# Two gated layers (state-space scan, quantised FFN, cross-attention, experts) on one core: ScalarE's order of key/value evictions and weight preparation, dummy matmuls at the start, one convolution tap on ScalarE

## The reference

```
x += tanh(g_xattn[0]) * L0_xattn(ctx, layernorm(x))   # in-projection 256->512, causal depthwise
                                                      # convolution (4 taps) + bias, SiLU, x/dt projections,
                                                      # softplus, 16-state scan over 512 steps, * SiLU(z)
x += tanh(g_ffn[0])   * L0_ffn(layernorm(x))          # gate/value/out weights quantised to {-1,0,1}*mean|w|,
                                                      # rows of activations rounded to 127 levels
x += tanh(g_xattn[1]) * L1_xattn(layernorm(x), ctx)   # 16 heads of 128, RMS-normed q and k, softmax, Wo
x += tanh(g_ffn[1])   * L1_ffn(layernorm(x))          # 4 experts, row n goes to expert n % 4, gated
```

## Time and profile before

| what | value |
|---|---|
| median of 3 runs | 1852.88 us (1848.29 to 1855.18) |
| the profiled execution | 1850.82 us |
| its span | 1849.0 us |
| TensorE busy | 1758.0 us (95%) |
| VectorE busy | 1317.9 us (71%) |
| ScalarE busy | 954.9 us (52%) |
| GpSimd busy | 662.6 us (36%) |
| DMA, mean over the span | 158 GB/s |

### The profile page before, as it was taken

The page is one execution under the profiler, slowest core; times in us unless marked ns, Lnnn a source line. Parts: engine busy times, 40 slices in busy tenths (PEclk is TensorE's granted clock), DMA queues, the critical chain, the costliest instruction groups (busy, mean ns, idle before and its releaser), DMA issues.

```text
span 1849.0 us, 19456 instructions
## 1 busy us (share of the span) xinstructions
PE 1758.0 (95%) x6086; PEld 802.9 (43%) x6086; DVE 1317.9 (71%) x1923; ACT 954.9 (52%) x1903; POOL 662.6 (36%) x696
## 2 busy tenths in 40 slices
PE   8989699979999999999999999999999899999999
PEld 3333244434444444444444444444444334455543
DVE  3999987989988798899797988987652444422221
ACT  5979956547554646566445566555435333330100
POOL 2244322246462335457322554562223333310000
PEclk9989899989999999999999999999999999999999
DMA  7999823787851157797213579732112799856210
GB/s 234 255 278 274 248 98 120 178 230 186 207 136 57 50 111 175 183 240 203 65 36 81 143 185 250 201 98 69 35 57 77 220 288 273 238 144 230 83 51 28
DMA packets 159046, 292.11 MB, mean 158 GB/s; under 512 B 18425, under 2 KB 51705, under 8 KB 156001
## 3 DMA queue, kind: packets, MB, share of 16 engines
q1 hardware_dynamic: 141664, 227.95, 39.1%
q0 software_dynamic: 17280, 62.92, 17.7%
HBM read 169.51 MB, written 58.26 MB: 123 GB/s over the span
## 4 chain that ended last, share of the span: by engine, by line
PE 65%; DVE 17%; ACT 6%; issue 5%; DMA 4%; POOL 2%; SPq 1%; DVEq 0%; ACTq 0%; POOLq 0%
PE p L830 10%; PE p L807 8%; PE p L790 8%; PE p L841 8%; PE p L877 6%; DVE s_M L1009 5%; PE p L813 4%; PE p L683 4%; PE p L892 3%; PE p L769 3%; PE p L764 3%; PE p L730 2%; DVE s_M L1004 2%; DVE s_M L1016 2%; DMA s_U<-in_Wq 1%
## 5 line engine op out<-in xcount | busy, mean ns | idle before, releaser
L1154 DVE CUSTOM_DVE_ANT_0 s_U<-p,s_U 128x512 f32<-128x512 f32 x256 | 187.2, 745 | 166.0 <-PE p L807 163.1
L1009 DVE TENSOR_TENSOR_SCAN s_M<-s_M 128x1024 f32<-128x1024 f32 x128 | 296.6, 2317 | 12.0 <-ACT s_M L1266 9.6
L807 PE MATMUL p<-s_U 128*128 128x512 f32 x512 | 267.0, 610 | 4.5 <-DVE s_U L1154 2.4
L790 PE MATMUL p<-s_U 128*128 128x512 f32 x512 | 253.7, 604 | 9.6 <-DMA s_U<-in_Wq 7.0
L1508 POOL DMA_DIRECT2D s_u<-s_M x120 | 113.3, 944 | 400.8 <-DVE s_M L1016 376.0
L1553 POOL TENSOR_SCALAR s_U<-s_U 128x512 f32<-128x512 f32 x256 | 228.6, 913 | 6.3
L841 PE MATMUL p<-s_U 128*128 128x512 f32 x512 | 223.9, 593 | 0.0
L830 PE MATMUL p<-s_U 128*128 128x512 f32 x472 | 213.5, 593 | 2.5 <-ACT s_U L1405 2.5
L1405 ACT COPY s_U<-p 128x512 f32<-128x512 f32 x196 | 105.6, 591 | 187.2 <-PE p L813 185.6
L1266 ACT ACTIVATE s_M<-s_dl,s_small 128x511 f32<-128x511 f32 x256 | 170.2, 717 | 44.2 <-DVE s_M L1009 39.7
L1400 ACT ACTIVATE s_U<-s_U 128x512 f32<-128x512 f32 x256 | 181.6, 710 | 5.3
(11 more groups left out here) (190 smaller groups left out, 2452.7 us busy)
## 6 DMA issues: line engine op xcount, KB each, us to landing
s_u<-s_M POOLq DMA_DIRECT2D x120, 512.0 KB, 7.6
s_bc<-bc_scratch SPq DMA_DIRECT2D x96, 256.0 KB, 4.5
k_scratch<-s_U SPq DMA_DIRECT2D x16, 1024.0 KB, 6.7
v_scratch<-s_U SPq DMA_DIRECT2D x16, 1024.0 KB, 7.4
s_U<-in_Wq SPq DMA_DIRECT2D x64, 256.0 KB, 7.2
s_U<-k_scratch SPq DMA_DIRECT2D x64, 256.0 KB, 5.2
s_U<-rk_scratch SPq DMA_DIRECT2D x64, 256.0 KB, 5.5
s_U<-in_Wo SPq DMA_DIRECT2D x64, 256.0 KB, 4.4
```

The costliest lines, as they stand in the source:

```text
L790: ins = e.matmul(banks[bk][:], wqq[j % 2][:, k, :], axT[b % 2][:, k, :], start=(k == 0), stop=(k == 3))
L807: e.matmul(banks[bk][:], qT[j % 3][:, k * 128:(k + 1) * 128], kT[j % 2], start=True, stop=True).then_inc(S["a_s"], 1)
L1009: e.tensor_tensor_scan(w, dA[i % 2], w, 0.0, ALU.mult, ALU.add).then_inc(S["m_s"], 1)
L1154: e.tensor_tensor_reduce(out=Pm[j % 2][:, k, :], in0=banks[ABANK[kind, j, k]][:], in1=rkb[j % 2], scale=rq[:, k:k + 1], scalar=-3.0e38, op ...
```

## The change: what it does

1. ScalarE's priorities become `AFMKQNE`: all of K, not its first 120 parts, goes ahead of Q, and Q ahead of N.
2. Written durations of some parts are set anew, and `plan()` takes TensorE as free from 7.0 on instead of 0.
3. The FFN's first part `e` no longer waits for all 12 `put`; TensorE's first `m` waits for the first 8, and the waits for all 12 go to the first out matmul and to the first VectorE product. The DMA of the bias rows is issued at `thr` of the last matrix instead of at the last Q part.
4. TensorE begins with 14 dummy matmuls of 128x128 by 128 columns in float32, after the second memset of GpSimd.
5. The convolution's unshifted tap and the bias are computed by ScalarE from PSUM (`Identity` with scale and bias), right after the copy; VectorE keeps three steps of four.

```
-            part((kind, i), [("PE", 1.75), ("ACT", 0.6)], ...)
+            part((kind, i), [("PE", 1.75), ("ACT", 1.25)], ...)
-            part((kind, i), [("DVE", 2.9)], ("in", i))
+            part((kind, i), [("DVE", 2.35)], ("in", i))
...
-                part(name, [("DVE", 2.3)], ("m", t, k - 1), free=pair)
+                part(name, [("DVE", 2.75 if k % 4 == 3 else 1.5)], ("m", t, k - 1), *([] if b else [(0, "put", 2, 3)]), free=pair)
-                part(name, [("PE", 2.6), ("ACT", 0.7)], ("e", t, 2), take=pair)
+                part(name, [("PE", 2.2), ("ACT", 0.7)], ("e", t, 2), *([] if b else [(0, "put", 1, 3)]), take=pair)
-                part(name, [("DVE", 1.0), ("POOL", 1.1)], ("yt", 3), *([] if b else [(0, "put", 2, 3)]))
+                part(name, [("DVE", 1.0), ("POOL", 1.1)], ("yt", 3), *([] if b else [(0, "bias", 0, 2)]))
...
-"s": [("PE", 0.86), ("DVE", 0.9)], "ex": [("ACT", 0.95 if k else 1.35)],  "rc": [("POOL", 1.03 if k else 1.2)]
+"s": [("PE", 0.86), ("DVE", 0.85)], "ex": [("ACT", 0.9 if k else 1.2)],   "rc": [("POOL", 0.95 if k else 1.3)]
...
-FIRST = {..., "ACT": "AFMLQNKE", ...}
+FIRST = {..., "ACT": "AFMKQNE", ...}
+    free["PE"] = 7.0
...
+            def warm():
+                e.wait_ge(S["p_set"], 2)
+                for _ in range(NWARM):                      # NWARM = 14
+                    e.matmul(banks[7][:, 0:128], onesf, onesf, start=True, stop=True)
...
                             if t == 0 and b == 0:
                                 e.wait_ge(S["d_rows"], 32)
-                                e.wait_ge(S["q_put"], 12)
+                                e.wait_ge(S["q_put"], 8)
...
                     elif kind == "l" and k == 3:
+                        if t == 0 and b == 0:
+                            e.wait_ge(S["q_put"], 12)
...
-                        e.tensor_scalar(ac[:, i, :], xs_[:, i, 0:512], cw[:, i, 0:1], cb[:, i:i + 1], ALU.mult, ALU.add).then_inc(*v.up())
-                        for k in range(1, 4):
+                        for k in range(3):
...
                     elif kind == "e" and k == 1:
                         if t == 0 and b == 0:
-                            e.wait_ge(S["q_put"], 12)
+                            e.wait_ge(S["d_rows"], 16)
...
                         e.wait_ge(S["f_th"], i + 1)
+                        if i == 0:
+                            e.wait_ge(S["q_put"], 12)
...
-                        e.copy(xs_[:, i, 3:515], banks[LBANK[b, "in", i]][:]).then_inc(S["m_xs"], 1)
+                        acc = banks[LBANK[b, "in", i]][:]
+                        e.copy(xs_[:, i, 3:515], acc)
+                        e.activation(ac[:, i, :], acc, ACT.Identity, bias=cb[:, i:i + 1], scale=cw[:, i, 3:4]).then_inc(S["m_xs"], 1)
...
-                    if (kind, w, c) == QUANT[-1]:
+                    if (kind, w, c) == ("thr", 2, 0):
                         e.wait_ge(S["q_row"], 1)
                         e.dma_start(brd, rows_).then_inc(S["d_rows"], 16)
```

More of the change, by code:

```diff
@@ L23 @@
 NW = 3
+NWARM = 14
 UW = 27744
@@ L224, in mamba @@
         if kind == "in":
-            part((kind, i), [("PE", 1.75), ("ACT", 0.6)], *([(b - 1, "yt", 3)] if b else []), take=own, free=own)
+            part((kind, i), [("PE", 1.75), ("ACT", 1.25)], *([(b - 1, "yt", 3)] if b else []), take=own, free=own)
         elif kind == "conv":
-            part((kind, i), [("DVE", 2.9)], ("in", i))
+            part((kind, i), [("DVE", 2.35)], ("in", i))
         elif kind == "silu":
@@ L249, in mamba @@
         elif kind == "mul":
-            part((kind, i), [("DVE", 1.25)], *([("out", i - NW)] if i >= NW else []), *([("bc", i // 2)] if b == 0 else []))
+            part((kind, i), [("DVE", 1.23)], *([("out", i - NW)] if i >= NW else []), *([("bc", i // 2)] if b == 0 else []))
         elif kind == "scan":
@@ L253, in mamba @@
         elif kind == "out":
-            part((kind, i), [("DVE", 1.27)] + ([("POOL", 0.8), ("SUM", 5.0)] if i < 2 * NS - 2 else []))
+            part((kind, i), [("DVE", 1.25)] + ([("POOL", 0.8), ("SUM", 5.0)] if i < 2 * NS - 2 else []))
         elif kind == "add":
@@ L347, in context @@
     for kind, j, k in ATTN:
-        does = {"q": [("PE", 0.86)] + ([("ACT", 1.3)] if k == 3 else []), "nq": [("PE", 0.35), ("ACT", 0.4)], "nt": [("PE", 0.2), ("ACT", 0.3), ("POOL", 1.1)], "s": [("PE", 0.86), ("DVE", 0.9)], "ex": [("ACT", 0.95 if k else 1.35)],
-                "rc": [("POOL", 1.03 if k else 1.2)], "tr": [("DVE", 0.65)], "mv": [("DMA", 2.5)], "mr": [("DMA", 4.0)], "t": [("PE", 0.56), ("ACT", 0.6)], "mx": [("PE", 1.73)], "mix": [("PE", 1.73 if halved("mix", j) else 3.45), ("ACT", 0.6)], "wx": [("PE", 1.73)], "w": [("PE", 1.73 if halved("w", j) else 3.45), ("DVE", 0.8)]}[kind]
+        does = {"q": [("PE", 0.86)] + ([("ACT", 1.3)] if k == 3 else []), "nq": [("PE", 0.35), ("ACT", 0.4)], "nt": [("PE", 0.2), ("ACT", 0.3), ("POOL", 1.1)], "s": [("PE", 0.86), ("DVE", 0.85)], "ex": [("ACT", 0.9 if k else 1.2)],
+                "rc": [("POOL", 0.95 if k else 1.3)], "tr": [("DVE", 0.65)], "mv": [("DMA", 2.5)], "mr": [("DMA", 4.0)], "t": [("PE", 0.56), ("ACT", 0.6)], "mx": [("PE", 1.73)], "mix": [("PE", 1.73 if halved("mix", j) else 3.45), ("ACT", 0.6)], "wx": [("PE", 1.73)], "w": [("PE", 1.73 if halved("w", j) else 3.45), ("DVE", 0.8)]}[kind]
         needs = {"q": [(j // NH, "xxt", 3)] + ([] if j else [("K", KV.index((NB - 1, 3, "n", 0)))]), "nq": [(NB, "q", j, 3)], "nt": [(NB, "nq", j, 0)], "s": [(NB, "nt", j, 0)] + ([] if j else [("K", len(KV) - 1)]) + ([(NB, "t" if on_pe(j - 2) else "tr", j - 2, 3)] if j > 1 else []), "ex": [(NB, "s", j, 3)], "rc": [(NB, "rc", j, k - 1) if k else (NB, "ex", j, 3)],
@@ L371, in experts @@
     return out
-FIRST = {"PE": "MNFAQKE", "DVE": "AFQMNKE", "ACT": "AFMLQNKE", "POOL": "MNAFQKE", "DMA": "QMNAFKE", "SUM": "MNAFQKE"}
+FIRST = {"PE": "MNFAQKE", "DVE": "AFQMNKE", "ACT": "AFMKQNE", "POOL": "MNAFQKE", "DMA": "QMNAFKE", "SUM": "MNAFQKE"}
 def plan():
@@ L411, in plan @@
                 ready = max([0.0] + [done[n] + 0.15 for n in needs] + [bank[x] for x in take])
-            key = max(ready, free[e]), FIRST[e].index("N" if s == "M" and name[0] else "L" if s == "K" and e == "ACT" and i < 120 else s)
+            key = max(ready, free[e]), FIRST[e].index("N" if s == "M" and name[0] else s)
             if best is None or key < best[0]:
@@ L898, in tensor @@
                        "K": pe_keys(), "A": pe_attn(), "E": pe_experts()}
+            warm()
             for s in order["PE"]:
@@ L964, in dve_mamba @@
                         e.wait_ge(S["m_xs"], 4 * b + i + 1)
[L965 to L966 removed]
+                        for k in range(3):
                             e.wait_ge(*v.now())
                             ins = e.scalar_tensor_tensor(ac[:, i, :], xs_[:, i, k:k + 512], cw[:, i, k:k + 1], ac[:, i, :], ALU.mult, ALU.add)
[L969 removed]
+                            ins.then_inc(*(v.up() if k < 2 else (S["m_ac"], 1)))
                     elif kind == "soft":
```

1 line of the change is left out of this document (removed).

## The result

The changed kernel takes 1855.34 us (median of 20 runs, 1848.49 to 1861.26), the kernel before 1849.35 (20 runs, 1841.46 to 1855.18). The ratio is 1.0029, 95% interval 1.0016 to 1.0043: slower by some 5 us. That is small, but the interval leaves out 1. The forecast was 1840 and a gain. The profiled execution has a span of 1856.1 us, against 1849.0.

The account below looks back on a forecast made before the run. TensorE, busy for 1758.0 of 1849.0 us, was taken as the bound. 1850.8 - 7 (first product) - 5 (to attention) = 1838.8, plus 2.1 for the runs' median, written 1840; own range 1831 to 1849, stated range 1822 to 1861.

Parts of the forecast that it names:

- Dummy matmuls: At the kernel's start: 28 dummy instructions end at 8.9 us, 1.8 late; gain 1.4 us, bounds 0.1 and 3.2.
- Convolution: Batch 0's four tiles on VectorE end near 21.4, 1.5 us earlier, passed on to the first scan; later batches count 0.
- So the FFN's row statistics can start 13.8 us earlier: Batch 0's state-space chain up to the first FFN: 1.5 + 8.9 + 3.4 us earlier, the upper bound of the gain.
- the first product starts near 257 and not at 264.38: First VectorE product of batch 0's FFN follows the last `put`, which ends near 256: gain 7 us.
- The stall moves: Rival, chance 0.23: last `put` ends near 264, FFN starts as before, TensorE's gain turns idle ahead of attention; 1850 us.
- 8.9 us that I had counted behind `thr`: VectorE's batch 0 chain loses 3.0 us to `thr`, 4.5 to four clips, 1.4 to waits; saved if Q moves behind.
- 3.4 us of transposes behind cold keys: Before the first FFN: TensorE transposes only from 241.25, behind low-clock keys, though VectorE's last product ends at 237.90.
- From there to attention: First FFN: TensorE's key work falls from 70.5 to about 47 us; shorter waits of 16 FFN parts gain 5 us.
- The gaps run cold: Rival, chance 0.07: with fewer keys to fill the FFN, TensorE waits in small pieces and runs at 1.2 GHz; 1847 us.
- ScalarE's backlog: Rival, chance 0.13: slow weight passes end at 275 or 287, first FFN product 11 to 23 us late; 1870 us.
- All of it comes back: Rival, chance 0.15: FFN follows the scan chain at once, TensorE is the only bound, 24 + 3 us off; 1826 us.
- Attention and later: From attention to the end, order changes only by durations: 0 us taken, bounds -25 and +25.

Follow-up runs that it names:

- after, two buffers: The changed kernel with a second buffer for the key norms' row that `nv` writes, order kept: 1850.86 us, ratio 0.9994 to the kernel before.
- after, old attention durations: The changed kernel with the old written durations of attention's scores, exponentials and reciprocals, one norms buffer: 1849.16 us, ratio 0.9997 to the kernel before.
- before, half keys: The kernel before, keys and values of the last 5 of 16 groups computed with one of two matmuls each: 1847.8 us, ratio 0.9987.
- the new order with the old waits: The kernel before with ScalarE's priority string AFMKQNE and nothing else: 1854.17 us, ratio 1.0019.
- the stalled kernel: The changed kernel with ScalarE's old priorities (keys ahead of weights for the first 120 parts only): 1850.46 us, ratio 1.0011 to the kernel before.

## Why the prediction was wrong, step by step

The table has the moments that the forecast was made of, in us, from one profile each (the first scan's start, the ends of the last gate part and of the last `put`, the starts of the first product and of the first q, and two lengths: first to last q, and from there to the last gate and up matmul).

| kernel | scan | gate | put | product | q | attention | last stage |
|---|---|---|---|---|---|---|---|
| before | 46.1 | 237.9 | 236.0 | 264.4 | 392.8 | 1217.5 | 220.3 |
| after | 41.1 | 238.8 | 257.8 | 265.9 | 395.3 | 1217.2 | 225.2 |
| after, two buffers | 39.2 | 228.7 | 247.7 | 255.8 | 384.5 | 1211.6 | 226.9 |
| after, old attention durations | 38.9 | 234.7 | 253.7 | 261.7 | 391.3 | 1216.0 | 222.0 |
| before, half keys | 45.0 | 238.2 | 236.3 | 264.7 | 395.9 | 1208.9 | 223.1 |

- **Dummy matmuls.** Right in kind, mis-sized: 1.4 us forecast, 3.2 measured (the group behind the in-projection starts at 13.75 instead of 16.97). The step that was off is the price "0.33 us for as much work as ran slow": the 28 instructions took 6.01 us. The Trainium skill's gap of 107 ns in TensorE: Matmul & The Clock Gate, section Back-to-back issue gap, gave an estimate of 6.0 and an end at 7.0; the trace agrees with it and not with my row of a lone weight load.
- **Convolution.** The four tiles end at 19.2, forecast 21.4. The Identity took 0.79 us (0.69 forecast) and VectorE's tiles 9.04 us in all. The tap's code moves the time by nothing, as counted. What I passed on to the first scan, 1.5 us, was 4.9, of which the dummy matmuls alone gave 3.5.
- **The step that failed:** "So the FFN's row statistics can start 13.8 us earlier", and with it "the first product starts near 257 and not at 264.38". The last `put` came as forecast (256; 257.8), so that half of the working was right, and "The stall moves" had it near 264. The first product came at 265.9 because the gate part that starts the FFN's chain was not earlier. In 15 of 16 profiles the first product follows the last gate part by 25.6 to 28.7 us, with the last `put` from 4 us before to 19 us after it; only the new order with the old waits has 37.4. So the finer waits did what they should, and the chain sets the start. It lost the 4.9 us of the start and the 8.9 us that I had counted behind `thr`: to the wait of 5.22 us behind late key weights, which the tap's durations bring, to the 6.20 behind ScalarE's `nv`, and to two clips of 1.2 us that still stand ahead of the last gate parts. The three sizes are read from one profile, and no run took the first or the last away. Of the 3.4 us of transposes behind cold keys, 2.3 were gained: 239.94, 1.1 us behind the gate.
- **What I had not looked at:** the queue of ScalarE behind a wait for a transfer. I weighed how long key evictions are, and not what they wait for. The single buffer of the norms was hidden at 0.72 us; `nv` waited 6.40, 2.74, 5.99 and 7.96 us in the four kernels with all the new durations and one buffer, and the two with a second buffer have no such wait. It is not the advanced keys that bring it: the 7.96 us are in the kernel with the old ScalarE order, and the new order with the old durations has no such wait near 200. With two buffers gate, product and q moved together by 10 to 11 us, and the ratio fell from 1.0029 to 0.9994, with intervals that don't touch. How much of it is the buffer is less sure. The gate part does not follow the length of the wait (2.74 and 5.99 us, 234.5 and 234.7), and the pair that differs by the buffer alone with attention's old durations has 234.7 and 234.0, and 0.9997 and 0.9981, 3 us, with intervals that overlap.
- **From there to attention,** "I take 5 us for the shorter waits of 16 FFN parts": nothing. The FFN took 128.4 us with 70.5 us of key work beside it, 129.4 with 52.5, and 131.2 with 34 us left out. TensorE "never idles" was true but for 4.5 us at the end, and meant nothing: the keys were filler. What sets the length is the chain through VectorE, ScalarE and TensorE's short FFN parts, and it depends on the order: three kernels with another order and more key work had 123.4 to 125.7.
- **The gaps run cold** was right as a mechanism: 16 instructions took 6.31 us behind the 9.73 us wait. VectorE, busy with batch 1, waited only 0.31 us for them, so most of the price was hidden there. The Trainium skill, TensorE: Matmul & The Clock Gate, section Why this matters for your kernels, warns of idle gaps between bursts, and the mean clock of 0.80 from 345 to 388 agrees. **ScalarE's backlog** did not come (257.8, not 275). **All of it comes back** fell with the half keys, and with the stalled kernel that is no slower.
- **Attention and later,** "Order changes only by durations. I take 0": 0 up to the last q (1217.2 against 1217.5), and 4.9 us in the last stage, by one part of the experts put behind a transfer. The wait itself is 2.94 us of it; where the other 2 lie was not read. Undoing attention's durations brought the changed kernel from 1.0029 to 0.9997. The upper bound of 25 us, which I thought wide, was nearly reached by other kernels: the tap's durations alone gave +24 and attention's alone +17 in the order of before. That the changed kernel, which has both, shows none of it up to the last q is luck of its order, and nothing in the forecast foresaw it.

Two slips in the forecast's numbers move nothing: 34 slots of 0.43 us are 14.6 us and not 14.7, and the four places named for TensorE's 91 us without work hold 68.8 of them, the other 22 lie behind 1400.

The profiled 7.1 us are +1.5 up to the first product, where -7.4 was forecast, +1.0 from there to q, where -5 was, -0.3 in attention and +4.9 in the last stage. Of the rivals "The stall moves" came nearest in time (1850), but not by its mechanism, since the last `put` was not late. "Attention as long as before", on which all rivals rest too, is itself loose: a first q 6.6 us late cost nothing at the last q in the run with the new priority alone. Open stays which moved part of the order costs the 24 and the 13 us in attention; the waits grew in many short pieces, and none was taken apart.

## What to carry to other kernels

An engine that is never idle is not the bound if part of its work can wait: leave half of that work out, or put its stall back, and see whether the end moves. When evictions are moved ahead, list what each of them waits for, transfers out of its target above all, and what stands behind it in its queue. Where written durations make the order, a changed duration is a change of its own: try it without the code, because here it cost 24 us where the code cost nothing.

## What the hardware showed that was not expected

- 28 plain float32 matmul instructions of 128 columns followed each other in 6.01 us at the start of the kernel, 0.215 us each, and in 5.40 to 6.16 us in the eight kernels that have them: the weight loads, of which a lone one took 0.33 us, were hidden.
- Four transfers of 512 float32 numbers each, issued behind a group's norms, kept their buffer busy so long that its next writer waited up to 7.96 us. In the stage where this was read, the changed kernel's DMA engines are busy for 0.93 of the time. In the order of before it was 0.72 us or nothing at the same place.
- Positions at 240 us scatter by 2 to 3 us either way among kernels that run the same order up to there (234.5 to 238.9 in three of them). What sets it was not looked into.
